# Results of seven slots of a mixture-of-experts layer, split in two 16-bit parts and turned by transposing transfers

## What is computed

```python
probs = jax.nn.softmax(x @ gate_w.T, axis=-1)
w, idx = jax.lax.top_k(probs, TOP_K)
w = w / jnp.sum(w, axis=-1, keepdims=True)
combine = jnp.zeros((T, E), x.dtype).at[jnp.arange(T)[:, None], idx].add(w)
def step(acc, inputs):
    gup, dn, ce = inputs
    g, u = jnp.split(x @ gup.T, 2, axis=-1)
    acc = acc + ce[:, None] * (jax.nn.silu(g) * u @ dn.T)
    return (acc, None)
```

## Time and profile before

| | us |
|---|---|
| device time, median of 3 runs | 549.48 |
| device time, lowest and highest | 548.71, 549.98 |
| device time of the profiled execution | 550.22 |
| span of the profiled execution | 548.4 |
| TensorE busy in the span | 494.8 |
| VectorE busy | 384.7 |
| ScalarE busy | 346.9 |
| GpSimd busy | 278.6 |

### The profile page before, as it was taken

How to read it: one execution, slowest core, us unless ns; L and a number is a source line. 1 busy time by engine, 2 the same in 40 slices (tenths; PEclk the granted TensorE clock), 3 DMA queues, 4 the chain that set the end, 5 groups by cost and what they waited for, 6 DMA issues and landing times.

```text
span 548.4 us, 12124 instructions
## 1 busy us (share of the span) xinstructions
PE 494.8 (90%) x3741; PEld 363.9 (66%) x3756; DVE 384.7 (70%) x797; ACT 346.9 (63%) x650; POOL 278.6 (51%) x356
## 2 busy tenths in 40 slices
PE   4976799999998888788899999999999999999980
PEld 3844456757675545435668988888888888777650
DVE  5664357987888766787678988887676767666551
ACT  2434569878889787485677777775666556545530
POOL 7333546554555454204217666575557655554244
PEclk9977879998999999799999999999999999999996
DMA  8667755866767543563666778866555566643224
GB/s 254 183 179 265 210 156 174 253 179 206 222 171 227 178 132 103 172 194 106 159 136 119 172 153 167 206 99 161 89 99 93 91 79 91 104 71 66 30 32 46
DMA packets 87883, 79.89 MB, mean 146 GB/s; under 512 B 48457, under 2 KB 73833, under 8 KB 87689
## 3 DMA queue, kind: packets, MB, share of 16 engines
q1 hardware_dynamic: 75900, 62.93, 42.1%
q0 software_dynamic: 11856, 16.16, 18.0%
q10 hardware_dynamic: 68, 0.03, 0.0%
HBM read 49.08 MB, written 22.41 MB: 130 GB/s over the span
## 4 chain that ended last, share of the span: by engine, by line
PE 65%; DVE 9%; DMA 8%; ACT 6%; SPq 5%; issue 4%; POOL 2%; DVEq 0%; ACTq 0%; POOLq 0%
PE bank L1543 28%; PE bank L1560 14%; PE bank L1347 5%; PE bank L1333 3%; PE bank L1298 3%; PE bank L1370 3%; SPq L489 2%; PE bank L1572 2%; DMA q_parts<-WE 2%; PE bank L1356 2%; DVE FB L1225 2%; PE bank L1314 2%; DVE FB L1221 2%; ACT FB L927 2%; DMA x_parts<-WE 2%
## 5 line engine op out<-in xcount | busy, mean ns | idle before, releaser
L1543 PE MATMUL bank<-FB,WE 128*128 128x0 bf16 x1440 | 187.8, 280 | 2.1 <-issue 0.8
L1543 PEld LDWEIGHTS bank<-FB,WE 128*128 x1440 | 136.1, 98 | 34.1 <-issue 3.3
L733 POOL DMA_INDIRECT out<-FB,slot_tok x60 | 99.8, 1664 | 88.5 <-DVE FB L1242 85.4
L927 ACT ACTIVATE FB<-FB 128x512 bf16<-128x512 f32 x120 | 75.6, 630 | 66.3 <-DVE FB L1221 65.9
L1225 DVE TENSOR_TENSOR FB<-FB 128x512 bf16<-128x512 f32 x120 | 83.4, 695 | 47.2 <-ACT FB L927 45.5
L1560 PE MATMUL bank<-FB,WE 128*128 128x0 bf16 x720 | 103.6, 280 | 2.6 <-DVE FB L1225 2.0
L1221 DVE TENSOR_TENSOR FB<-FB,bank 128x512 f32<-128x512 f32 x120 | 82.1, 684 | 23.6 <-ACT FB L921 22.0
L724 POOL DMA_INDIRECT FB<-x_parts,slot_tok x60 | 61.8, 1029 | 68.4 <-DMA FB<-FB 27.5
L921 ACT ACTIVATE FB<-bank 128x512 f32<-128x512 f32 x120 | 71.0, 592 | 30.9 <-PE bank L1543 28.7
L1560 PEld LDWEIGHTS bank<-FB,WE 128*128 x720 | 67.8, 98 | 21.3 <-issue 5.6
L649 POOL TENSOR_TENSOR WE<-FB,WE 128x256 bf16<-128x256 f32 x104 | 67.7, 678 | 25.3 <-ACT WE L764 25.3
(11 more groups left out here) (186 smaller groups left out, 621.4 us busy)
## 6 DMA issues: line engine op xcount, KB each, us to landing
FB<-w SPq DMA_DIRECT2D x26, 512.0 KB, 5.7
WE<-w SPq DMA_DIRECT2D x44, 256.0 KB, 3.2
WE<-q_parts SPq DMA_DIRECT2D x32, 200.0 KB
WE<-x SPq DMA_DIRECT2D x16, 256.0 KB, 5.7
q_parts<-FB SPq DMA_DIRECT2D x32, 128.0 KB
x_parts<-WE SPq DMA_DIRECT2D x20, 128.0 KB, 4.3
out<-WE SPq DMA_DIRECT2D x20, 128.0 KB, 5.4
q_parts<-WE SPq DMA_DIRECT2D x16, 128.0 KB
```

The lines of the kernel that those rows point to most:

```text
L733: pool.indirect_dma_start(out=out, out_offset=bass.IndirectOffsetOnAxis(ap=slot_tok[:, c:c + 1].bitcast(U32), axis=0), in_=result_tile(c), ...
L927: nc.scalar.activation(hT[k % 3][:, 0, :], hid[k % 2], ACT.Copy).then_inc(hi_ready, 1)
L1543: ins = nc.tensor.matmul(to, wf[:, bass.ds(at + o, P)], xgT[s % 2][:, 2 * part + kc, :].shape_from_register(long[s % 2]), start=(z == 0), ...
```

## The change

For slots 6 to 12 (`BY_DMA`) TensorE turns no results. Instead ScalarE writes the high parts of the result (`result_hi`) and VectorE the low parts (`result_lo`, high part subtracted from the bank) into `y_parts`, which is the memory of `yT` seen as 16-bit values. Both are done in chunks 1 and 2 of the next slot, and it is now `result_lo` that raises `yT_ready`. SyncE turns both parts of a tile by one transposing transfer (`turn_result`) into `y_sb[i]`. ScalarE then writes the high part times the weight into `turn_bank` (`weighted_hi`, chunks 5, 6, 7 and chunk 0 of the slot after), and VectorE multiplies the low part with the weight and adds the two (`result`, chunks 6, 7, and 0 and 1 of the slot after). There are four result buffers instead of two; the two new ones take the place of the third buffer of `hT` from slot 6 on, so that `hidden_hi(k)` waits for `down` of k - 2 instead of k - 3. The semaphores `y_out` are one for each tile of a slot.

```diff
+BY_DMA = range(6, NS - 2)
...
+            def turn_result(s, i):
+                c = SUB * s + i
+                for kc in range(KC):
+                    sp.wait_ge(yT_ready[kc], s + 1)
+                result_tile_free(sp, c)
+                sp.dma_start(y_sb[i].bitcast(BF16).rearrange("p (k f) -> p k f", k=2 * KC), y_parts[:, i], transpose=True).then_inc(y_turned[i], 16)
...
                     for i in range(2):
                         turn_tile(s + 1, 2 * half + i)
+                    if s - 1 in BY_DMA:
+                        for i in range(2):
+                            turn_result(s - 1, 2 * half + i)
...
+            def result_hi(s, kc):
+                act.wait_ge(d_mm, FC * (s + 1))
+                y_parts_free(act, s)
+                nc.scalar.activation(y_parts[:, :, kc, :], y_bank(s, kc).rearrange("p (i f) -> p i f", i=SUB), ACT.Copy).then_inc(yh_ready, 1)
+
+            def weighted_hi(c):
+                act.wait_ge(y_turned[c % SUB], 16 * (BY_DMA.index(c // SUB) + 1))
+                act.wait_ge(y_ready, c)
+                nc.scalar.activation(turn_bank[:, c % 2 * D:(c % 2 + 1) * D], y_sb[c % SUB].bitcast(BF16)[:, 0:D], ACT.Copy,
+                                     scale=slot_w[:, c:c + 1]).then_inc(yw_ready, 1)
...
                     if c in (1, 2) and s > 0:
-                        yT_copy(s - 1, c - 1)
+                        if s - 1 in BY_DMA:
+                            result_hi(s - 1, c - 1)
+                        else:
+                            yT_copy(s - 1, c - 1)
+                    if c in (5, 6, 7) and s - 1 in BY_DMA:
+                        weighted_hi(SUB * (s - 1) + c - 5)
+                    if c == 0 and s - 2 in BY_DMA:
+                        weighted_hi(SUB * (s - 1) - 1)
...
+            def result_lo(s, kc):
+                dve.wait_ge(yh_ready, KC * BY_DMA.index(s) + kc + 1)
+                nc.vector.tensor_tensor(y_parts[:, :, KC + kc, :], y_bank(s, kc).rearrange("p (i f) -> p i f", i=SUB), y_parts[:, :, kc, :], ALU.subtract).then_inc(yT_ready[kc], 1)
...
             def result(c):
-                dve.wait_ge(yt_mm, c // 2 + 1)
+                if c // SUB in BY_DMA:
+                    dve.wait_ge(yw_ready, c - SUB * BY_DMA[0] + 1)
+                    nc.vector.scalar_tensor_tensor(out=y_sb[c % SUB], in0=y_sb[c % SUB].bitcast(BF16)[:, D:2 * D], scalar=slot_w[:, c:c + 1],
+                                                   in1=turn_bank[:, c % 2 * D:(c % 2 + 1) * D], op0=ALU.mult, op1=ALU.add).then_inc(y_ready, 1)
+                    return
...
-                    if c in (4, 5, 7) and 0 < s < NS - 1:
+                    if s - 1 in BY_DMA:
+                        if c in (1, 2):
+                            result_lo(s - 1, c - 1)
+                        if c in (6, 7):
+                            result(SUB * (s - 1) + c - 6)
+                    elif c in (4, 5, 7) and 0 < s < NS - 1:
                         result(SUB * (s - 1) + (4, 5, 7).index(c))
-                    if c == 0 and s > 1:
+                    if s - 2 in BY_DMA:
+                        if c < 2:
+                            result(SUB * (s - 2) + 2 + c)
+                    elif c == 0 and s > 1:
                         result(SUB * (s - 1) - 1)
...
-                    if c == 3 and s > 0:
+                    if c == 3 and s > 0 and s - 1 not in BY_DMA:
                         turned_result(s - 1, 0)
-                    if c == (6 if s < NS - 1 else 5) and s > 0:
+                    if c == (6 if s < NS - 1 else 5) and s > 0 and s - 1 not in BY_DMA:
                         turned_result(s - 1, 1)
```

More of the change, by code:

```diff
@@ L193, in moe_attention_kernel @@
         yT = ffb(KC * CAP).rearrange("p (k n) -> p k n", k=KC)
-        y_sb = [ffb(D) for _ in range(2)]
+        y_parts = yT.rearrange("p k n -> p (k n)").bitcast(BF16).rearrange("p (i k f) -> p i k f", i=SUB, k=2 * KC)
+        y_sb = [ffb(D) for _ in range(2)] + [hT[2].rearrange("p s n -> p (s n)")[:, 2 * D * i:2 * D * (i + 1)].bitcast(F32) for i in range(2)]
         spare = carver(FB[:, 7680:13312], 5632)
@@ L315, in moe_attention_kernel @@
         y_ready = sem("y_ready")
+        yh_ready = sem("yh_ready")
+        y_turned = [sem(f"y_turned{i}") for i in range(SUB)]
+        yw_ready = sem("yw_ready")
         dve_step = sem("dve_step")
@@ L330, in moe_attention_kernel @@
         late_lo = sem("late_lo")
-        y_out = [sem(f"y_out{p}") for p in range(2)]
+        y_out = [sem(f"y_out{i}") for i in range(SUB)]
         xg_in = [sem(f"xg_in{p}") for p in range(2)]
@@ L439, in result_tile, with result_tile_free, h_buffer, h_before @@
         def result_tile(c):
-            return xg[c % 2].bitcast(F32) if LAST <= c < LAST + 2 else y_sb[c % 2]
+            return xg[c % 2].bitcast(F32) if LAST <= c < LAST + 2 else y_sb[c % (SUB if c >= SUB * BY_DMA[0] else 2)]
+        def result_tile_free(engine, c):
+            before = c - (SUB if c >= SUB * BY_DMA[0] + 2 else 2)
+            if before >= 0:
+                engine.wait_ge(y_out[before % SUB], 16 * (before // SUB + 1))
+        def h_buffer(k):
+            return k % 3 if k < FC * BY_DMA[0] else k % 2
+        def h_before(k):
+            return next((j for j in range(k - 1, -1, -1) if h_buffer(j) == h_buffer(k)), None)
+        def turned_by_pe(s):
+            return 2 * (s - sum(n < s for n in BY_DMA))
+        def y_parts_free(engine, s):
+            if s - 1 in BY_DMA:
+                for i in range(SUB):
+                    engine.wait_ge(y_turned[i], 16 * (BY_DMA.index(s - 1) + 1))
+            elif s > 0:
+                engine.wait_ge(yt_mm, turned_by_pe(s))
         @block.sync
@@ L752, in _ @@
                 scatter(SUB * (NS - 1) + i)
-            for p in range(2):
-                pool.wait_ge(y_out[p], 8 * NTP)
+            for i in range(SUB):
+                pool.wait_ge(y_out[i], 16 * NS)
         @block.scalar
@@ L1559, in down @@
                         last = c == FC - 1 and wpart == 1
[L1560 removed]
+                        ins = nc.tensor.matmul(to, wf[:, bass.ds(at + o, P)], hT[h_buffer(k)][:, part, :].shape_from_register(long[s % 2]),
                                                start=first, stop=last, skip_group_check=True)
```

29 lines of the change are left out of this document (13 added, 16 removed).

## The result

| | before | after |
|---|---|---|
| device time, median of 15 runs | 549.48 us | 554.55 us |
| profiled execution, device time | 550.22 us | 557.18 us |
| its span | 548.4 us | 555.4 us |

The ratio is 1.0085, with a 95% interval from 1.0054 to 1.0115: the change makes the kernel slower by 4.7 us (3 to 6.3). The forecast was 2.0 us slower. The ratio is taken from runs in the fast state alone (one run of the changed kernel, 560.57 us, was in the slower one), so it differs a little from the quotient of the two medians, which lie 5.1 us apart.

A forecast was written before the change was run, and what follows sets the result against it. TensorE was taken to bound the kernel from 280 us on. Span 548.4 - 6.2 (transposes) + 6.4 (debt on ScalarE) + 1.8 (late transfers) = 550.4 us, on the median 551.5 us; range 546.5 to 556.0.

The forecast's parts named there:

- What bounds the kernel, and what the transposes are worth: TensorE bounds from 280 us on; removing 14 groups of transposes in seven slots, 0.44 us each, gains 6.2 us.
- Edits at no cost: Beside other work: result_hi, result_lo, two-operand result and two-buffer hT were to add no time on the path.
- The rounds on ScalarE: Chunks 6, 7, 0: hidden_hi waits behind weighted_hi for result; rounds of about 2.7 us make result_lo late, sum 6.4 us.
- The page on ScalarE: weighted_hi writing to PSUM: by the page each copy would be 0.04 us shorter, some 0.5 us over the kernel.
- The transfers: Seven slots: slow transfers delay TensorE by 1.4 us in one slot of five for each of two kinds, about 1.8 us.
- the margin: Before a slot's first up: room for the fourth input tile to land falls from some 5 us to 0.7.
- Gain: Rival: smaller ScalarE debt or no wait for yT_ready[0]; 547.4 us at half debt and delay, 545 without debt; chance 0.20.
- Late input tiles: Rival: slower gathers and turns make first up and third weighted_hi wait, 1 us in six slots, 555.7 us; chance 0.17.

The follow-up runs named there:

- each order alone: Changed kernel with weighted_hi moved behind hidden_hi: ratio to before 1.0009; changed kernel with both pairs of gathers ahead of the scatter on GpSimd's queue: 1.0074.
- both together: Changed kernel with weighted_hi behind hidden_hi and the gathers first on GpSimd's queue: ratio to before 0.9929, 545.6 us.

## Why the prediction was right in kind and short in size

- **What bounds the kernel, and what the transposes are worth.** Right. 14 x 0.44 = 6.2 us were forecast; the slots give 6.1, the ratio 5.3.
- **Edits at no cost.** Right for the two buffers of `hT` (128.7 us with and without). `result_hi`, `result_lo` and the two-operand `result` last 0.59, 0.68 and 0.47 us against 0.60, 0.69 and 0.48 forecast.
- **The rounds on ScalarE.** The mechanism, its place and its end were right: TensorE waits in chunk 2, for `result_lo`, in slots 8 to 12, with less in 12 and 13. The size was not: 6.4 us were forecast and the run without transfers shows 8.8. A small part of it stands in chunk 1, where `down` waits for `hidden_lo` of chunk 7; the prediction had no wait there. The term that failed is the duration of `weighted_hi` and its handovers. It was taken at 0.42 us with 0.31 held; it lasts 0.48, `hidden_hi` starts 0.42 behind its start, and it starts 0.10 after `result` ends and not 0.03. This makes a round 2.84 us instead of 2.68. Three rounds add 0.5 a slot, and the wait that was worked out to end 10.0 us after `silu(6)` ends at 10.6. In the run without transfers slots 8 to 11 are 1.9, 1.7, 1.7 and 2.1 us longer than without transposes, where 1.5, 1.2, 1.3 and 1.5 were forecast, and slots 12 and 13 are 1.0 and 0.45 longer instead of 0.8 and 0.1. The prediction had this inside its bounds (10 us with 0.1 more in each new step). For the duration it had taken the longer of its two rows, and for the handover that of steps without a weight for each row; both were still too short.
- **The page on ScalarE.** "ScalarE: Activation LUTs" of the Trainium skill (step-by-step section) calls PSUM the lower-latency destination. It gives no figure; the 0.04 us that the prediction put on it is the difference of two rows that differ in their source. This form of copy, from 16-bit SBUF to a bank with a scale for each partition, lasts 476 ns where the SBUF row has 419. So the copy did not become shorter, but no run here tests the page's sentence: whether the scale, the 16-bit source or the destination makes it longer was not separated.
- **The transfers.** 1.8 us were forecast, and the changed kernel has 1.2 us more than the one without them, which the intervals don't tell from none. The forecast's own terms don't give 1.8 either: 1.4 us in one slot of five, over seven slots, is 2.0 us for one kind of transfer and 3.9 for both. That it fits is luck. That the margin is used up, and what uses it up, a gather that lands after 5 us, is shown by the run without a copy. What I had not seen is the packets that the slow landings go with, and how the two costs lie on each other: the rounds lengthen the slot by 1.7 us and so give the input tiles that much more time. As soon as the rounds go, the tiles cost 4 to 5 us (1.0009 against 0.9929 with the copy moved: 4.4 us; 127.7 against 122.6 with no copy: 5.1 us).
- **The rivals.** *Gain* failed, as the wait for `yT_ready[0]` is there in every slot. *Late input tiles* was there too, but as the second of two: on the changed kernel it is worth about 1 us at most (0.6 by the gathers moved, 1.2 by the transfers left out, neither told from none). The deciding quantity was whether late tiles come more often than in one slot of five. In both profiles of the changed kernel two slots start late by them, 10 and 12, by 0.2 to 1.1 us.

With the measured terms the sum reads -5.3 + 8.7 + 1.2 = +4.6 us, against +4.7 by the ratio. The three terms are differences of ratios along one row of kernels, so that they add up is no check of its own. What supports them is where TensorE waits in each profile.

## What to carry to other kernels

When an engine in a loop of several engines is given a new small step, what it waits for and what stands behind it in the queue can count for more than its length. Here 28 copies of 0.48 us cost 4 us more in one place than one instruction further on. Put a step that waits for a side path behind the step that the critical path wants from this engine. The place has a price too: with the results turned later, the same copy held up `silu` for 2.6 us from its place behind `hidden_hi`. And when a change gives back its gain, look for a second give-back behind the first: each order alone brought 4.2 and 0.6 us, both together 8.6.

## What the runs showed of the hardware

- A transposing transfer of 128 rows of 512 16-bit values takes SyncE 1.2 us to issue.
- A gather that usually lands in 2.8 us (median of the earlier trace rows) took a median of 3.0 beside such transfers of results, and 4.2 where a 16 KB packet of the `instruction` queue fell into the same time as well (17 of 30 took more than 4.0 us; with only one of the two beside them 3 of 95 did).
- A copy by ScalarE of 256 elements from 16-bit SBUF to a bank, with a scale for each partition, lasts 476 ns, and the next step starts 410 to 420 ns after its start.
- ScalarE once stood for 2.4 us in front of a `silu` whose matmuls had ended, in the first profile of the changed kernel and not in the second. The cause is not known.
